# Query projection of 16-head cross-attention in three fp16 passes instead of one fp32 product

## The chip, the cores and the metric

The kernel runs on one core of a Trainium2 chip. One launch computes a whole twelve-stage model. The metric is the device time of the launch in microseconds (us). TensorE (PE) does the matrix products, VectorE (DVE) and ScalarE (ACT) the elementwise work, GpSimd (POOL) side work, and SyncE (SP) issues the transfers.

## The reference, cut to what matters

Three of the twelve stages (L0, L2 and L3 xattn) are the same cross-attention with different weights. Two batches of 128 tokens attend to 2048 context rows each. There are 16 query heads and 8 key heads, of 128 values each.

```
xn = layernorm(x)                                  # [2, 128, 256]
q = xn @ Wq;  k = ctx @ Wk;  v = ctx @ Wv          # k and v repeated for two heads each
scores = einsum('bhtd,bhsd->bhts', q, k) / sqrt(128)
attn = softmax(where(mask, scores, -inf))
x = x + einsum('bhts,bhsd->bhtd', attn, v) ... @ Wo
```

Between them stand nine other stages (state-space layers, other attentions, feed-forward layers). The last one, L3 ffn, has eight experts whose weights are quantised in advance, during the L2 and L3 xattn stages.

## The kernel before, in words

`xattn_layer` (lines 291 to 840) builds one cross-attention stage. It never forms k: the query of a head is multiplied by Wk's transpose (`qk_project`, L449), and the scores are that product against the transposed context, which stays in SBUF as an fp16 high part and an fp16 low part. A product with both parts takes three passes: high by high, high by low, low by high (`PARTS`, line 36).

The 16 heads go in four bodies (i = 0 to 3) of four heads. A head has two units, one per batch, so a body has eight units u = 0 to 7. Two heads share one key head and form a group (i, j), j = 0 or 1. In unit (i, u) PE does, in this order:

- `mix_high` (L475): high part of the probabilities by the low part of the values, 16 products of 128x128;
- `tail_out` (L523) of an earlier head, in odd units;
- `q_project` (L442) for group (i+1, 0) in u = 2 and (i+1, 1) in u = 6, of bodies 0 to 2: four fp32 products of 128x256, two trace records each;
- `scores` (L462) of unit u + 3: 12 products of 128x512 fp16;
- `tail_values` (L518) in even units, which waits for `oT` from DVE (L757);
- `mix_both` (L484): 16 products of 128x256 fp16;
- `qk_project` (L449) of the group, in u = 2 and 6.

The projections of (0, 0) and (0, 1) stand ahead of the bodies (lines 563 to 571), and after them PE has `scores` of units 0, 1 and 2 and nothing else before `mix_high` of unit 0.

DVE adds the mask, takes maxima (L742), inverts the sums (L752) and makes the low part of the probabilities (L766). ACT does the exponentials (L597), the high part (L612) and the copies of the projections out of PSUM (L587, L591).

The probabilities must be turned before they are mixed. That is done by transposing DMAs on SP's queue: `turn_high` (L379) and `turn_low` (L386) for each unit. SP executes its program in order, and in the same program it issues the weight loads: `load_q(i, j)` (L367, columns 0 to 639, Wq and Wk of a group) and `load_v` (L371). Each has a wait ahead of it, so whatever stands behind a wait of SP stands still until that wait ends. `turn_high` of unit u waits for `mix_both` of unit u - 2, since two buffers are used in turn; for u = 0 and 1 of body 0 it waits only for ACT's probabilities. Before, the loads stood so:

```
if u == 0 and not final:
    sp.wait_ge(s.qk_psum, 2 * i + 1)
    load_q(i + 1, 0)
if u == 4 and not final:
    sp.wait_ge(s.qk_psum, 2 * i + 2)
    load_q(i + 1, 1)
```

`qk_psum` counts finished `qk_project`s: group (i, j) makes it 2i + j + 1.

GpSimd in the L0 stage sets constants and makes the low part of the values (L702). In L2 and L3 it runs `experts_pool` (L3193): for each body one expert, whose first half is L3204 and L3207 (after DVE's L3153, in unit 0) and whose second half is L3211 to L3226 (after DVE's L3161, in unit 3).

Of the kernel before, what the change touches and what calls it, by code (L numbers as in the profile page):

```python
# [22 lines left out]
P = 128  # L23
# [46 lines left out]
def begin(nc, stack, dram):  # L70
    k = Shared()
    k.nc, k.dram = nc, dram

    def sb(name, shape, dt=F32):
        return stack.enter_context(nc.sbuf_tensor(name, shape, dt))

    k.x = sb("x", [P, B, D])
    k.xn = sb("xn", [P, B, D])
    k.xnT = sb("xnT", [P, DC, T])
    k.ident = sb("ident", [P, P])  # L80
    k.identb = sb("identb", [P, P], BF16)
    k.identh = sb("identh", [P, P], F16)
    k.ones = sb("ones", [P, P])
    k.zeros = sb("zeros", [P, 2 * D])
    k.zero = sb("zero", [P, 1])
    k.causal = sb("causal", [P, P])
    k.upper = sb("upper", [P, P])
    k.hm = sb("hm", [P, 16])
    k.wsum = sb("wsum", [P, 2])
    k.bits = sb("bits", [P, 2], I32)  # L90
    k.stats = sb("stats", [P, B, 6])
    k.mv = sb("mv", [P, B, 2])
    k.std = sb("std", [P, 2, B])
    k.rstd = sb("rstd", [P, 2, B])

    k.ctx = sb("ctx", [P, 2, B * KT, CD], F16)
    k.ctxT = sb("ctxT", [P, 2, B, CTX], F16)
    k.arena = [sb(f"arena{i}", [P, ARENA]) for i in range(2)]
    k.ps = stack.enter_context(nc.psum_tensor("ps", [P, 8, 512], F32))

    k.psh = k.ps[:].rearrange("p a n -> p (a n)").bitcast(F16).rearrange("p (a n) -> p a n", a=8)
    k.psi = k.ps[:].rearrange("p a n -> p (a n)").bitcast(I32).rearrange("p (a n) -> p a n", a=8)
    k.g = semaphores(nc, stack, "g", "x_loaded first_w0 first_w1 mask_loaded keys_loaded0 keys_loaded1 values_loaded0 values_loaded1 "
                               "keys_high0 keys_high1 keys_low0 keys_low1 values_high0 values_high1 values_low const_id const_zero const_ones const_copied "
                               "var_ready std_ready xn_ready xnT_psum xnT_ready dve_chain act_chain pool_chain "
                               "w_loaded0 w_loaded1 out_stored ln_chain "
                               "raw_loaded w_exp w_scaled w_bits w_added w_coded w_turned codes_loaded scale_rows")
    free = [i for i in range(256) if nc.free_contains(i)]
    k.turns = [range(max(free) + 1 - SEMS[0], max(free) + 1),
               range(max(free) + 1 - SEMS[0] - SEMS[1], max(free) + 1 - SEMS[0])]  # L110
    k.dve_n = k.act_n = k.pool_n = 0
    k.w_count = [0, 0]

    k.ln = k.xt = 0
    return k
# [175 lines left out]
def xattn_layer(k, name, slot, loaded, stage_loads):  # L291
# [8 lines left out]
    with ExitStack() as stack:  # L300
        def sb(nm, shape, dt=F32):
            return stack.enter_context(nc.sbuf_tensor(f"{name}_{nm}", shape, dt))
        s = semaphores(nc, stack, name, "wq0 wq1 wv0 wv1 out_done qT_psum qT_ready qk_psum qk_high qk_ready s_ready "
                 "s_read0 s_read1 p_ready r_raw r_ready p_high p_low t_hi0 t_hi1 t_lo0 t_lo1 mixed "
                 "oT_ready oh_psum oh_ready mask_ready last_psum last_hi last_lo0 last_lo1 oT_low", k.turns[slot])
        w = k.arena[slot][:, 0:2 * GW].rearrange("p (a n) -> p a n", a=2)
        bias = sb("bias", [P, B, CTX], BF16)
        anyone = sb("anyone", [P, B])
# [5 lines left out]
        pp = k.arena[slot][:, 2 * GW + 2 * CTX:2 * GW + 4 * CTX].bitcast(F16).rearrange("p (s a n) -> p s a n", s=2, a=2)  # L314
        pt = k.arena[slot][:, 2 * GW:2 * GW + 2 * CTX].bitcast(F16)\
            .rearrange("p (s a t q) -> p s a t q", s=2, t=KT, a=2)
        qT = sb("qT", [P, 2, T])
        qk = sb("qk", [P, 2, 2, 2, T], F16)
        mx = sb("mx", [P, 2, 2])
# [6 lines left out]
            weigh = Weigh(sb("round", [P, WE]), sb("exp", [P, FE // 2, WE // BLK]), sb("inv", [P, FE // 2, WE // BLK]))  # L326
        oT = sb("oT", [P, T])
        oh = sb("oh", [P, T])
        wq = [w[:, i, 0:2 * DC * HD].rearrange("p (h c d) -> p h c d", h=2, c=DC) for i in range(2)]
        wkT = [w[:, i, 512:640] for i in range(2)]  # L330
        wv = [w[:, i, 640:768] for i in range(2)]
        wo = [w[:, i, 768:768 + 2 * D].rearrange("p (h d) -> p h d", h=2) for i in range(2)]
# [30 lines left out]
        with nc.Block() as block:  # L363
            @block.sync
            def _(sp):
# [30 lines left out]
                def body(i, first, final):  # L396
                    for u in range(UNITS):
                        early = first and u < 2
                        if u == 0 and not final:
                            sp.wait_ge(s.qk_psum, 2 * i + 1)  # L400
                            load_q(i + 1, 0)
                        if u == 4 and not final:
                            sp.wait_ge(s.qk_psum, 2 * i + 2)
                            load_q(i + 1, 1)
                        if u == 3 and not first:
                            sp.wait_ge(s.out_done, BODY * i)
                            load_v(i, 1)
# [13 lines left out]
            def _(pe):  # L421
# [3 lines left out]
                keep_busy(k, 1, 3 if opening else 4, still)  # L425
                xT_tensor(k, pe, k.xn, 0, n)
                keep_busy(k, 1, 5, still)
                pe.wait_ge(g.xnT_ready, k.xt + 1)

                def q_project(i, j, first):  # L430

                    if first and opening:
                        pe.wait_ge((g.first_w0, g.first_w1)[j], 16)
                    elif first:
                        wait_weights(k, pe, slot, loaded)
                    else:
                        pe.wait_ge(wq_sem[j], 16 * i)
                    if not (first and j == 0):
                        pe.wait_ge(s.qk_ready, 2 * i + j)
                    for h in range(2):  # L440
                        for c in range(DC):
                            last = nc.tensor.matmul(PREP[:, h * T:(h + 1) * T], wq[j][:, h, c, :], k.xnT[:, c, :],  # L442
                                                    start=(c == 0), stop=(c == DC - 1))
                    last.then_inc(s.qT_psum, 1)

                def qk_project(i, j):
# [132 lines left out]
            @block.scalar  # L579
            def _(act):  # L580
                ln_scalar(k, act, n)
                xT_scalar(k, act, k.xnT, 0)
                nc.scalar.activation(unused[:], k.zero[:], ACT.Exp, bias=k.zero[:])

                def q_copy(i, j):
# [107 lines left out]

            @block.gpsimd
            def _(pool):
                if opening:
                    constants_pool(k, pool)
                    for b, done in enumerate((g.values_high0, g.values_high1)):
                        pool.wait_ge(done, 1)
                        for half in range(2):  # L700
                            at = slice(half * CTX // 2, (half + 1) * CTX // 2)
                            nc.gpsimd.tensor_tensor(rows_of(1, b)[:, at], raw_context(k, b)[1][:, at], rows_of(0, b)[:, at],  # L702
                                                    ALU.subtract).then_inc(g.values_low, 1)
                if experts is not None:
                    experts_pool(k, pool, weigh, experts)

            @block.vector
            def _(dve):
                if opening:
                    dve.wait_ge(g.x_loaded, 16)  # L710
                ln_vector(k, dve, k.x, k.xn, LN_EPS, n)
                if opening:
                    dve.wait_ge(g.mask_loaded, 16)
                else:
# [2475 lines left out]
    k.dve_n = chain.n  # L3190

def experts_pool(k, pool, w, first):  # L3193

    nc, g = k.nc, k.g
    chain = Chain(pool, g.pool_chain, k.pool_n)
    blocks = WE // PIECES // BLK

    for e in range(first, first + FE // 2):
# [6 lines left out]
        for j in range(PIECES):  # L3206
            nc.gpsimd.tensor_tensor(in_blocks(y[j]), in_blocks(y[j]), each_block(inv[j]), ALU.mult)\  # L3207
                .then_inc(g.w_scaled, 1)
        pool.wait_ge(g.w_bits, e + 1)
        for j in range(PIECES):  # L3210
            nc.gpsimd.tensor_scalar(y[j], y[j], E4M3_TOP, -E4M3_TOP, ALU.min, ALU.max)  # L3211
# [13 lines left out]
        for j in own:  # L3225
            nc.gpsimd.tensor_tensor(in_blocks(coded[j]), in_blocks(y[j]), each_block(ex[j]), ALU.mult)\  # L3226
                .then_inc(g.w_coded, 1)
    k.pool_n = chain.n

def turn_experts(k, sp, own):
# [523 lines left out]
```

## Time and profile before

| what | value |
|---|---|
| three timed runs | 1295.93, 1300.39, 1302.8 us, median 1300.39 |
| profiled execution, own time | 1297.31 us |
| its span in the trace | 1295.6 us |
| PE matmul busy | 1146.9 us, 89% of the span |
| DVE busy | 992.0 us, 77% |
| ACT busy | 860.9 us, 66% |
| POOL busy | 317.5 us, 25% |
| mean granted TensorE clock | 0.959 of full speed |

The span is 1.7 us shorter than the execution's own time, and that execution is 3.1 us below the median. The three cross-attention stages lie at about 3 to 240 us, 597 to 835 us and 970 to 1200 us.
### The profile page before, as it was taken

To read this page: it belongs to the slowest core of one execution; us is meant where nothing else is said; L and a number is where in the kernel's file an instruction comes from. 1 tells how busy PE (TensorE), PEld (TensorE's weight loads), DVE (VectorE), ACT (ScalarE), POOL (GpSimd) and SP (SyncE) were. 2 spreads that over 40 slices of the span, in tenths; PEclk is the share of its full clock that TensorE was granted. 3 is DMA by queue.
4 is the path that set the end of the run, shared out by engine and by line. 5 is a ranking of instruction groups with operands and counts; after the bars stand their busy time and mean duration, and the time that the engine had idled before them with its cause. 6 is when DMAs were issued, how large, how long until landed. Compare 5 with 4: busy or idle time off the path is not lost. (4 is left out here: it accounts for less than half of the span.)

```text
span 1295.6 us, 23108 instructions
## 1 busy us (share of the span) xinstructions
PE 1146.9 (89%) x8738; PEld 761.3 (59%) x8742; DVE 992.0 (77%) x1858; ACT 860.9 (66%) x1303; POOL 317.5 (25%) x353
## 2 busy tenths in 40 slices
PE   7999999848776887899899999887998999999987
PEld 3677676635322444486566666645874666666644
DVE  6788878297768883493899989776987998998654
ACT  5777778484454887422877777565976777777563
POOL 3000000100362000000172654502650456275200
PEclk8899999959986999899899999999998999999999
DMA  7999999201374000901899999514745999999600
GB/s 280 172 186 189 188 171 187 84 1 74 82 146 82 2 3 2 245 25 59 162 200 182 206 182 169 130 43 160 205 115 129 180 181 183 178 163 169 123 1 9
DMA packets 450833, 170.00 MB, mean 131 GB/s; under 512 B 437160, under 2 KB 437544, under 8 KB 449064
## 3 DMA queue, kind: packets, MB, share of 16 engines
q1 hardware_dynamic: 450736, 168.72, 62.3%
q8 instruction: 60, 0.98, 0.3%
q14 instruction: 37, 0.30, 0.1%
HBM read 58.84 MB, written 0.26 MB: 46 GB/s over the span
## 5 line engine op out<-in xcount | busy, mean ns | idle before, releaser
L462 PE MATMUL ps<-ctxT,L_xattn_qk 128*128 128x512 f16 x1152 | 270.3, 385 | 0.8 <-DVE L_xattn_mx L742 0.5
L766 DVE SCALAR_TENSOR_TENSOR arena<-L_xattn_sm,L_xattn_rr,arena 128x1024 f16<-128x1024 f32 x192 | 260.9, 1399 | 9.4 <-ACT arena L612 9.4
L597 ACT ACTIVATE L_xattn_sm<-L_xattn_sm,L_xattn_mx 128x2048 f32<-128x2048 f32 x96 | 192.3, 2003 | 75.6 <-DVE L_xattn_mx L742 73.9
L612 ACT ACTIVATE arena<-L_xattn_sm,L_xattn_rr 128x1024 f16<-128x1024 f32 x192 | 210.0, 1140 | 5.2
L462 PEld LDWEIGHTS ps<-ctxT,L_xattn_qk 128*128 128x128 f16 x1152 | 112.5, 99 | 130.1 <-issue 9.9
L484 PE MATMUL ps<-arena,ctx 128*128 128x256 f16 x1488 | 177.7, 273 | 0.0
L484 PEld LDWEIGHTS ps<-arena,ctx 128*128 128x128 f16 x1488 | 145.4, 98 | 31.9
L742 DVE CUSTOM_DVE_ANT_0 L_xattn_sm<-ps,L_xattn_bias 128x1024 f32<-128x1024 f32 x96 | 117.0, 1219 | 55.7 <-issue 55.5
L742 DVE CUSTOM_DVE_ANT_0 L_xattn_sm<-ps,L_xattn_bias,L_xattn_mx 128x1024 f32<-128x1024 f32 x96 | 123.2, 1284 | 2.4 <-DVE L_xattn_mx L742 2.1
L475 PE MATMUL ps<-arena,ctx 128*128 128x128 f16 x1488 | 100.8, 222 | 9.6 <-DMA arena<-arena 9.5
L475 PEld LDWEIGHTS ps<-arena,ctx 128*128 128x128 f16 x1488 | 92.3, 99 | 25.1 <-DMA arena<-arena 13.4
L2794 DVE TENSOR_REDUCE L_xattn_mx<-ps 128x1 f32<-128x512 f32 x128 | 81.0, 684 | 19.6 <-PE ps L2350 18.2
L180 PE MATMUL ps<-ctxT,identh 128*128 128x512 f16 x312 | 80.8, 394 | 8.6 <-PEq L363 2.5
L602 ACT ACTIVATE L_xattn_rr<-L_xattn_raw,L_xattn_anyone 128x1 f32<-128x1 f32 x96 | 28.2, 294 | 74.7 <-DVE L_xattn_raw L752 73.7
L2624 ACT ACTIVATE L_xattn_p<-ps,zero 128x512 f32<-128x512 f32 x84 | 53.1, 685 | 9.7 <-PE ps L2379 9.3
L180 PEld LDWEIGHTS ps<-ctxT,identh 128*128 128x128 f16 x312 | 29.6, 100 | 46.3 <-issue 22.5
L3211 POOL TENSOR_SCALAR arena<-arena 128x384 f32<-128x384 f32 x32 | 26.5, 827 | 119.9 <-DVE L_xattn_round L3161 118.4
L147 ACT ACT_TABLE_LOAD x10 | 12.8, 1283 | 63.7 <-PEq L892 20.3
L1940 PE MATMUL ps<-L_ffn_hTp,L_ffn_parts 128*128 128x256 f16 x408 | 51.1, 277 | 2.1 <-DVE L_ffn_parts L2041 2.1
L899 POOL MEMSET L_attn_xcp<- 128x524 f32 x1 | 0.5, 537 | 210.9 <-POOLq L363 210.9
L3212 POOL TENSOR_SCALAR L_xattn_round<-L_xattn_round 128x384 f32<-128x384 f32 x32 | 49.5, 1548 | 2.0
L3204 POOL TENSOR_TENSOR L_xattn_inv<-bits,L_xattn_exp 128x48 int32<-128x48 int32 x8 | 2.1, 266 | 190.5 <-DVE L_xattn_exp L3153 190.5
(585 smaller groups left out, 2082.7 us busy)
## 6 DMA issues: line engine op xcount, KB each, us to landing
L_ffn_ring<-in_L_ffn_experts SPq DMA_DIRECT2D x34, 384.0 KB, 3.6
arena<-in_L_xattn_w SPq DMA_DIRECT2D x36, 320.0 KB, 3.7
arena<-in_L_ffn_experts SPq DMA_DIRECT2D x8, 768.0 KB, 7.7
arena<-in_L_xattn_w SPq DMA_DIRECT2D x6, 640.0 KB, 6.5
arena<-arena SPq DMA_TRANSPOSE x193, 4.5
arena<-in_L_ffn_codes SPq DMA_DIRECT2D x1, 3072.0 KB, 11.2
arena<-in_L_attn_w SPq DMA_DIRECT2D x1, 2163.0 KB, 19.3
arena<-in_L_attn_w SPq DMA_DIRECT2D x2, 1026.0 KB, 5.1
```

The costliest lines, as they stand in the source:

```text
L180: k.nc.tensor.matmul(k.ps[:, bank, :], k.identh[:], k.ctxT[:, 0, 0, 0:512] if data is None else data, start=True, stop=True)
L462: last = nc.tensor.matmul(ps[:, at, :], qk[:, h // 2, qp, h % 2, b * P:(b + 1) * P], k.ctxT[:, cp, b, at * 512:(at + 1) * 512], start=(a = ...
L475: nc.tensor.matmul(O[h][:, b, 0, :], k.ctx[:, 1, b * KT + kt, :], pt[:, b, 0, kt, :], start=(kt == 0), stop=False, skip_group_check=True)
L484: last = nc.tensor.matmul(O[h][:, b, :, :], k.ctx[:, 0, b * KT + kt, :], pt[:, b, :, kt, :], start=False, stop=(kt == KT - 1), skip_group_ ...
L597: nc.scalar.activation(sm[:, u % 2, :], sm[:, u % 2, :], ACT.Exp, bias=mx[:, u % 2, 1:2], scale=-1.0, accum_out=rs[:, u % 2:u % 2 + 1]).th ...
L612: nc.scalar.mul(pp[:, u % 2, 0, at], sm[:, u % 2, at], rr[:, u % 2:u % 2 + 1]).then_inc(s.p_high, 1)
L742: nc.vector.tensor_tensor_reduce(sm[:, u % 2, half * 1024:(half + 1) * 1024], ps[:, 2 * half:2 * half + 2, :].rearrange("p a n -> p (a n)" ...
L766: nc.vector.scalar_tensor_tensor(pp[:, u % 2, 1, at], sm[:, u % 2, at], rr[:, u % 2:u % 2 + 1], pp[:, u % 2, 0, at], ALU.mult, ALU.subtrac ...
L1940: last = nc.tensor.matmul(gu(e)[:, half * T:(half + 1) * T], w13(e, wp)[:, c, half * MI:(half + 1) * MI], hTp[:, hp, c, :], start=(c == 0 ...
L2624: nc.scalar.activation(pt[step % 3][:, j, :, :].rearrange("p i q -> p (i q)"), ps[:, ST_BANK[piece % 3], :], ACT.Exp, bias=k.zero[:], scal ...
L2794: nc.vector.tensor_reduce(mx[:, G % 2, 2 * pair + which, at:at + 1], ps[:, bank, :], AX_X, ALU.max)\
L3212: last = nc.gpsimd.tensor_scalar(r[j], r[j], E4M3_LOW, ROUND, ALU.max, ALU.mult)
```

## The change: what it does, and the diff

- The normalised, transposed input is split into an fp16 high part (ACT, in place of the fp32 copy) and an fp16 low part (a new DVE subtraction out of PSUM) before the first projection.
- The query weights of each group are split into high and low fp16 parts in a new tile `wqh`, by a copy and a subtraction of 128x512 on GpSimd, eight groups per stage (`split_queries`).
- `q_project` does three fp16 passes (12 products of 128x256) and waits for GpSimd's `wq_low` and not for the load.
- `load_q` is issued earlier: (i+1, 1) in u = 0 and (i+2, 0) in u = 4, and (1, 0) and (1, 1) both in u = 0 of body 0. The waits ahead of them are those on `qk_psum` of the group that used the buffer before.
- In L2 and L3 the splits of later groups stand inside `experts_pool`: (e+1, 1) behind the scaling, (e+2, 0) at an expert's end (e counted within the stage).

```diff
@@ SyncE
+                        if u == 0 and first:
+                            sp.wait_ge(s.qk_psum, 1)
+                            load_q(1, 0)
                         if u == 0 and not final:
-                            sp.wait_ge(s.qk_psum, 2 * i + 1)
-                            load_q(i + 1, 0)
-                        if u == 4 and not final:
                             sp.wait_ge(s.qk_psum, 2 * i + 2)
                             load_q(i + 1, 1)
+                        if u == 4 and i + 2 <= LASTI:
+                            sp.wait_ge(s.qk_psum, 2 * i + 3)
+                            load_q(i + 2, 0)
@@ TensorE
-                pe.wait_ge(g.xnT_ready, k.xt + 1)
+                pe.wait_ge(g.xn_low, {"L0_xattn": 1, "L2_xattn": 2, "L3_xattn": 3}[name])
                 def q_project(i, j, first):
...
+                    pe.wait_ge(s.wq_low, 2 * i + j + 1)
...
                         for c in range(DC):
-                            last = nc.tensor.matmul(PREP[:, h * T:(h + 1) * T], wq[j][:, h, c, :], k.xnT[:, c, :],
-                                                    start=(c == 0), stop=(c == DC - 1))
+                            for a, (wpart, xp) in enumerate(PARTS):
+                                last = nc.tensor.matmul(PREP[:, h * T:(h + 1) * T], wq[j][:, wpart, h, c, :],
+                                                        xh[:, xp, c, :], start=(c == 0 and a == 0),
+                                                        stop=(c == DC - 1 and a == len(PARTS) - 1))
@@ ScalarE
-                xT_scalar(k, act, k.xnT, 0)
+                act.wait_ge(g.xnT_psum, k.xt + 1)
+                nc.scalar.copy(xh[:, 0, :, :].rearrange("p c t -> p (c t)"), ps[:, 0, :]).then_inc(g.xnT_ready, 1)
@@ GpSimd
+                def split_queries(chain, i, j):
+                    if i == 0 and opening:
+                        pool.wait_ge((g.first_w0, g.first_w1)[j], 16)
+                    elif i == 0:
+                        wait_weights(k, pool, slot, loaded)
+                    else:
+                        pool.wait_ge(wq_sem[j], 16 * i)
+                        pool.wait_ge(s.qT_psum, 2 * i + j - 1)
+                    chain(nc.gpsimd.tensor_copy(wqh[:, j, 0, :], w[:, j, 0:2 * DC * HD]))
+                    nc.gpsimd.tensor_tensor(wqh[:, j, 1, :], w[:, j, 0:2 * DC * HD], wqh[:, j, 0, :], ALU.subtract)\
+                        .then_inc(s.wq_low, 1)
                 if opening:
                     constants_pool(k, pool)
+                chain = Chain(pool, g.pool_chain, k.pool_n)
+                split_queries(chain, 0, 0)
+                if opening:
                     for b, done in enumerate((g.values_high0, g.values_high1)):
+                        if b:
+                            split_queries(chain, 0, 1)
                         pool.wait_ge(done, 1)
...
+                    for i in range(1, LASTI + 1):
+                        for j in range(2):
+                            split_queries(chain, i, j)
+                else:
+                    split_queries(chain, 0, 1)
+                    split_queries(chain, 1, 0)
+                    experts_pool(k, pool, chain, weigh, experts, split_queries)
@@ VectorE
                 ln_vector(k, dve, k.x, k.xn, LN_EPS, n)
+                dve.wait_ge(g.xnT_ready, k.xt + 1)
+                nc.vector.tensor_tensor(xh[:, 1, :, :].rearrange("p c t -> p (c t)"), ps[:, 0, :],
+                                        xh[:, 0, :, :].rearrange("p c t -> p (c t)"), ALU.subtract).then_inc(g.xn_low, 1)
@@ experts_pool, for e in range(first, first + FE // 2)
                 .then_inc(g.w_scaled, 1)
+        if e % 4 < LASTI:
+            split_queries(chain, e % 4 + 1, 1)
         pool.wait_ge(g.w_bits, e + 1)
...
                 .then_inc(g.w_coded, 1)
+        if e % 4 + 1 < LASTI:
+            split_queries(chain, e % 4 + 2, 0)
```

## Rows read from the trace of the kernel before

**Rows 1.** Windows in L0 and L2: PE, PEld, DVE, ACT, POOL busy; clock, DMA share, GB/s.

```profile
45.00:208.00 163.00, 163.00 (x1234) 114.62 (x1233) 133.14 (x244) 126.60 (x163) 0.00 (x0) 1.00 1.00 183
630.00:793.00 163.00, 160.59 (x1204) 111.27 (x1202) 147.12 (x245) 122.60 (x157) 83.95 (x75) 1.00 0.98 186
```

**Rows 2.** PE's timeline (start, length in us), L0 stage, units 1 to 4 of body 0.

```profile
46.12 1.91 PE L484 MATMUL ps<-arena,ctx 128*128 128x256 f16 x16
47.87 1.06 PE L475 MATMUL ps<-arena,ctx 128*128 128x128 f16 x16
48.76 1.95 PE L442 MATMUL ps<-xnT,arena 128*128 128x256 f32 x8
50.54 2.75 PE L462 MATMUL ps<-ctxT,L_xattn_qk 128*128 128x512 f16 x12
...
55.31 1.02 PE L449 MATMUL ps<-L_xattn_qT,arena 128*128 128x512 f32 x2
...
62.32 0.89 PE L475 MATMUL ps<-arena,ctx 128*128 128x128 f16 x13
```

**Rows 3.** Timeline of the opening of L2: SP's first turn, and PE.

```profile
617.07 1.68 SPq L379 DMA_TRANSPOSE arena<-arena  x1
...
617.56 1.13 PE L449 MATMUL ps<-L_xattn_qT,arena 128*128 128x512 f32 x2 [1.31 <-ACT L_xattn_qT L587]
621.63 1.89 PE L475 MATMUL ps<-arena,ctx 128*128 128x128 f16 x16 [2.94 <-DMA arena<-arena]
```

**Rows 4.** The same timeline in the opening of L0.

```profile
29.92 2.04 SPq L379 DMA_TRANSPOSE arena<-arena  x1
...
30.42 1.12 PE L449 MATMUL ps<-L_xattn_qT,arena 128*128 128x512 f32 x2 [0.23 <-ACT L_xattn_qT L587]
```

**Rows 5.** Window behind that wait in L2; columns as in Rows 1.

```profile
621.60:627.60 6.00, 5.97 (x27) 3.27 (x28) 4.18 (x7) 5.42 (x6) 0.00 (x0) 0.51 1.05 182
```

**Rows 6.** SP: query loads; landing of all 93 high turns; one turn behind a load.

```profile
L367 SPq DMA_DIRECT2D arena<-in_L_xattn_w x18: 328/928/1290, 17.3 to 1121.6; - x18
...
DMA to landing us min/median/max: 4.3/4.6/6.5
...
L379 SPq DMA_TRANSPOSE arena<-arena x1: 3146/3146/3146, 134.4 to 134.4; - x1
...
DMA to landing us min/median/max: 6.4/6.4/6.4
```

**Rows 7.** Timeline of L2's and L0's starts; DVE's L727 by line (ns min/median/max).

```profile
600.08 0.59 ACT L196 COPY xnT<-ps 128x512 f32<-128x512 f32 x1 [1.72 <-PE ps L190]
...
602.88 0.59 ACT L587 COPY L_xattn_qT<-ps 128x512 f32<-128x512 f32 x1 [0.61 <-PE ps L442]
...
14.61 0.58 ACT L587 COPY L_xattn_qT<-ps 128x512 f32<-128x512 f32 x1
...
L727 DVE SCALAR_TENSOR_TENSOR L_xattn_qk<-ps,L_xattn_qk x24: 675/682/692, 18.0 to 1159.9; 128x512 f16<-128x512 f32 x24
```

**Rows 8.** Timeline of L2, body 0, unit 2 and the unit behind it.

```profile
634.15 4.19 POOL L3207 TENSOR_TENSOR arena<-arena,L_xattn_inv 128x384 f32<-128x384 f32 x4
...
636.34 3.09 DVE L766 SCALAR_TENSOR_TENSOR arena<-L_xattn_sm,L_xattn_rr,arena 128x1024 f16<-128x1024 f32 x2
...
639.42 0.40 DVE L757 SCALAR_TENSOR_TENSOR L_xattn_oT<-ps,L_xattn_oT 128x256 f32<-128x256 f32 x1
...
639.98 0.41 PEld L518 LDWEIGHTS ps<-L_xattn_oT,arena 128*128 128x128 f32 x2
...
642.36 2.48 DVE L766 SCALAR_TENSOR_TENSOR arena<-L_xattn_sm,L_xattn_rr,arena 128x1024 f16<-128x1024 f32 x2
```

**Rows 9.** GpSimd: groups by line nearest in shape to a split; L0's opening (timeline).

```profile
L2291 POOL TENSOR_TENSOR L_xattn_p<-L_xattn_p 128x512 f16<-128x512 f32 x16 | 18.9, 1184 | 0.0
L2290 POOL COPY L_xattn_p<-L_xattn_p 128x512 f16<-128x512 f16 x16 | 10.0, 626 | 32.7 <-ACT L_xattn_p L2554 32.5
...
19.89 9.31 POOL L702 TENSOR_TENSOR ctx<-arena,ctx 128x1024 f16<-128x1024 f32 x4 [15.62 <-ACT ctx L675]
```

More of the change, by code:

```diff
@@ L104, in begin @@
                                "keys_high0 keys_high1 keys_low0 keys_low1 values_high0 values_high1 values_low const_id const_zero const_ones const_copied "
-                               "var_ready std_ready xn_ready xnT_psum xnT_ready dve_chain act_chain pool_chain "
+                               "var_ready std_ready xn_ready xnT_psum xnT_ready xn_low dve_chain act_chain pool_chain "
                                "w_loaded0 w_loaded1 out_stored ln_chain "
@@ L304, in xattn_layer @@
                  "s_read0 s_read1 p_ready r_raw r_ready p_high p_low t_hi0 t_hi1 t_lo0 t_lo1 mixed "
-                 "oT_ready oh_psum oh_ready mask_ready last_psum last_hi last_lo0 last_lo1 oT_low", k.turns[slot])
+                 "oT_ready oh_psum oh_ready mask_ready last_psum last_hi last_lo0 last_lo1 oT_low wq_low", k.turns[slot])
         w = k.arena[slot][:, 0:2 * GW].rearrange("p (a n) -> p a n", a=2)
@@ L316, in xattn_layer @@
             .rearrange("p (s a t q) -> p s a t q", s=2, t=KT, a=2)
+        xh = flat(k.xnT[:]).bitcast(F16).rearrange("p (a c t) -> p a c t", a=2, c=DC)
+        wqh = sb("wqh", [P, 2, 2, 2 * DC * HD], F16)
         qT = sb("qT", [P, 2, T])
@@ L328, in xattn_layer @@
         oh = sb("oh", [P, T])
-        wq = [w[:, i, 0:2 * DC * HD].rearrange("p (h c d) -> p h c d", h=2, c=DC) for i in range(2)]
+        wq = [wqh[:, i, :, :].rearrange("p a (h c d) -> p a h c d", h=2, c=DC) for i in range(2)]
         wkT = [w[:, i, 512:640] for i in range(2)]
@@ L427, in _ @@
                 keep_busy(k, 1, 5, still)
-                pe.wait_ge(g.xnT_ready, k.xt + 1)
+                pe.wait_ge(g.xn_low, {"L0_xattn": 1, "L2_xattn": 2, "L3_xattn": 3}[name])
                 def q_project(i, j, first):
[L432 to L437, printed above, removed]
+                    pe.wait_ge(s.wq_low, 2 * i + j + 1)
                     if not (first and j == 0):
@@ L703, in _ @@
                                                     ALU.subtract).then_inc(g.values_low, 1)
-                if experts is not None:
-                    experts_pool(k, pool, weigh, experts)
+                    for i in range(1, LASTI + 1):
[5 more added lines that the diff above has]
+                    experts_pool(k, pool, chain, weigh, experts, split_queries)
+                k.pool_n = chain.n
             @block.vector
@@ L3190, in expert_end, with experts_pool @@
     k.dve_n = chain.n
-def experts_pool(k, pool, w, first):
+def experts_pool(k, pool, chain, w, first, split_queries):
     nc, g = k.nc, k.g
-    chain = Chain(pool, g.pool_chain, k.pool_n)
     blocks = WE // PIECES // BLK
@@ L3227, in experts_pool @@
                 .then_inc(g.w_coded, 1)
-    k.pool_n = chain.n
+        if e % 4 + 1 < LASTI:
+            split_queries(chain, e % 4 + 2, 0)
 def turn_experts(k, sp, own):
```

## The prediction
> **What bounds the kernel now.** I read the windows first. In the middle of the L0 cross-attention PE is busy 163.00 of 163.00 us at full clock, DVE 133; in L2 PE has 160.59 of 163 and DVE 147 [rows 1]. So inside these three stages PE is the bound, with about 1.5% of idle time in L2 and L3, and whatever PE issues there costs its own spacing. The DMA engines' share is 1.00 there too, so transfers have little room. The second view is PE's timeline [rows 2], where one block starts as the last ends. The third is the opening of a stage [rows 3, 4]. There PE runs dry: after L449 it has nothing until the first turned probabilities land, and L475 waits 2.94 us for that DMA. The first L475 follows SP's first turn by 4.56 us (617.07 to 621.63), so in an opening SP's issue time sets PE's restart.
>
> **The projections in the bodies (gain).** From L442's start to L462's start are 50.54 - 48.76 = 1.78 us for the fp32 form. The nearest fp16 row of the same width is L484: 16 products from 46.12 to 47.87, 109 ns each [rows 2]. Twelve of these are 1.31 us. A projection saves 0.47 us. There are two per body in bodies 0 to 2 of three stages, 18 in all, each between busy PE blocks: 18 x 0.47 = 8.5 us. Bounds: nothing, if what follows waits anyway, and 24 x 0.47 = 11.3 if the six opening projections counted too.
>
> **The six opening projections.** Group (0, 1) saves nothing: L449 behind it waits for ACT's copy [rows 3]. In L0 this projection has a new wait, on a split that stands behind two of the four L702, so from about 19.89 + 9.31 / 2 = 24.5 us on. By L2290 and L2291 a split is 0.63 + 1.18 = 1.8 us [rows 9], ready at 26.4. The projection and three units' scores must be done when L449's input comes at 30.42 [rows 4], and 26.4 + 1.31 + 12 x 0.216 (the spacing of 2.75 us of L462) = 30.3 just fits: 0, with 0.5 as the upper bound. Group (0, 0) gets DVE's subtraction in its way: ACT ends at 600.67, DVE adds about 0.68 by L727 with the same output shape and PSUM source, PE takes 1.31 and 0.2 of latency, so ACT's copy starts near 602.9 to 603.1, against 602.88 [rows 7]. I take +0.2 in L2 and in L3. In L0 that copy starts only at 14.61, behind ACT's key copy, so split and subtraction are covered there; were the keys earlier, 2 us would show. The splits of L2 and L3 for (0, 0) run while DVE normalises; their weights are loaded a stage ahead. Sum: +0.4.
>
> **SP's new wait in the opening (loss).** Body 0, unit 0 now has a wait for qk_psum >= 2 and load (1, 1) ahead of turn_high(0, 0). Two is reached when the L449 of group (0, 1) ends: 617.56 + 1.13 = 618.69 in L2, 30.42 + 1.12 = 31.54 in L0 [rows 3, 4]. A load takes SP 0.33 us on an idle queue, 0.93 by the median [rows 6]. The turn then goes out near 619.1 in place of 617.07, and 32.0 in place of 29.92: 2.0 us later. I take the same for L3, whose lines are L2's. The 320 KB of the load are in flight with it: the turn at 134.36 right behind a load took 6.4 us to land, the median turn 4.6 [rows 6]; I add 0.3, bounded by 0 and 1.8. Behind the waiting instruction stand all turns of the stage, and PE waits for the first. Its idle time of 2.94 becomes 5.2 us. Cost 3 x 2.3 = +6.9 us, and nothing of that is won back, since PE is the bound afterwards. Bounds 3 and 12, which includes the clock: behind the wait PE works 6 us at 0.51 of full speed, the lower level (1.2 GHz) [rows 5]. If full clock comes back at the same moment as before, half of the delay falls on slow time and the cost is 3.5; if it comes back one such stretch's half later (3 us at half speed), each opening costs 1.5 more.
>
> **SP's waits in the bodies (loss).** In unit 4 of bodies 0 and 1, and unit 0 of bodies 1 and 2, SP waits for the L449 of two units before, which stands directly behind the L484 that the next turn waits for anyway. Before, that load was issued in SP's free time. Now: L449 ends 55.31 + 1.02 = 56.33, the load is 0.93, so the turn goes at 57.3; with 4.6 to landing 61.9, with 6.4 it is 63.7. PE wants it at 62.32 [rows 2, 6]. So a usual landing has 0.4 us of slack and a slow one is 1.4 late. With a load right ahead of each I take 0.2 us on the mean, 12 times: +2.4, bounded by 0 and 12 x 1.0 = 12. The load in unit 4 of body 2 disappears, worth nothing: its turn has slack.
>
> **GpSimd beside DVE.** A split costs 1.8 us [rows 9], 24 are 43 us on an engine with 25% of its time used; no wait for wq_low is late in a body, since the loads are two to four units earlier than the use. What it slows is DVE: L766 takes 3.09 us beside GpSimd's L3207 and 2.48 without [rows 8]. In L2, unit 2 of body 0, L757 ends at 639.82 and PE's L518 starts at 639.98 [rows 8]. That 0.16 us of slack means that of the 0.47 saved 0.3 is waited there; and the new split (1, 1) directly behind L3207 lengthens the same L766 by up to 0.3 more. I take 0.6 for that unit and 0.1 for body 2's, in two stages: +1.4, bounded by 0 and 4. The Trainium skill's GPSIMD Engine Reference, section Key points, states that GpSimd shares its SBUF interfaces with VectorE and that a DVE instruction with two SBUF inputs contends; by that rule the LN and score passes (L742, one input in PSUM) would be untouched. The trace agrees as far as L766 goes. In L0 DVE has 30 us of idle time in 163 [rows 1], so there it costs nothing.
>
> **The sum.** -8.5 + 0.4 + 6.9 + 2.4 + 1.4 = +2.6 us. Against the profiled execution's own 1297.3 us that is 1299.9; that execution is 3.1 below the median of the runs, so on the median 1300.4 the forecast is **1303.0 us**. A measurement of this kernel tells a change from none at about 0.5%, 6.5 us; by that the forecast is no change.
>
> **The rivals.**
> *Late turns (slower).* The place is SP's program order at the twelve waits in the bodies. Its price is the landing of a turn with 320 KB ahead of it. It decides from the point where issue to landing exceeds 62.32 - 57.3 = 5.0 us. For it: DMA share 1.00 [rows 1], 6.4 us behind a load, maximum 6.5 [rows 6]. Against it: median 4.6. At 6.0 us each is 1.0 late, 12 us instead of 2.4: 1303.0 + 9.6 = 1312.6. Chance 0.23.
> *The opening is nearly free (faster).* The first landing is not what holds PE: the later turn falls where the clock is low anyway, the slack of 0.4 us holds at the twelve places, and DVE is not slowed. Then -8.5 + 0.4 + 1.5 = -6.6, 1293.8 us. For it: 6 us at 0.51 clock [rows 5]. Against it: 2.94 us of idle time put down to exactly that DMA, and nothing else for PE to do. Chance 0.08.
> *The fp16 form is not 109 ns a product.* Each product needs its own weight load, twelve in place of eight records; if the spacing were L442's own 0.22 us, a projection would take 2.7 us and 18 would cost 16 us, 1328. L484 has the same shape and one load per product at 109 ns, so I give it 0.02. The Trainium skill's page TensorE: Matmul & The Clock Gate, section Back-to-back issue gap, puts an isolated product of 256 columns at 256 / 2.4 + 2.5 = 109 ns, which is the trace's number.
> *The forecast,* openings 2.3 us each and small waits at the turns: 0.67.
>
> **How the numbers follow.** The forecast case spans 1297 to 1309 by its bounds taken together (openings 3.5 to 10, turns 0 to 5), and most of it lies within 6.5 us of 1300.4; about a twentieth of all lies above and belongs to slower. Faster by over 0.5% is 0.07, slower 0.25, no change 0.68. The range of 8 in 10 goes from 1294 to the middle of the late-turn case, 1312.
>
> **What would show it.** Right: L442's successor takes 12 records at 109 ns, 1.3 us from start to the next L462; the first L475 of each stage waits about 5 us on the DMA in place of 3, its turn issued 0.3 to 0.5 us after L449's end with the load between; in the bodies the turns of units 4 and 0 go out about 1.7 us after L449's start. Wrong: first turns at the old distance behind ACT's L612; L475 waiting over 1 us on a DMA at many of the twelve places (late turns); PE's wait for wq_low visible; or L518's waits for L757 grown past 1.5 us each.

## The result, and the profile after

The changed kernel takes 1310.46 us (median of 5 runs, 1307.10 to 1312.76); the kernel before, on the same chip, 1299.33. The ratio is 1.0080 with a 95% interval of 1.0055 to 1.0105: slower by about 10 us, where the forecast said 2.6 slower and called it no change (less than 0.5%). The profiled execution has a span of 1308.7 us against 1295.6, at a mean granted clock of 0.954 against 0.959. So the traces differ by 13.1 us, 3 more than the timed runs. Of the 13.1, the three cross-attention stages hold 9.2 (710.4 us before, 719.6 after) and the nine stages that the change doesn't touch 3.9; the experiments show what a granted clock does to such stages.

The page of the changed kernel: the engines' busy time, and L477, which is L475 of before (columns: busy us, mean ns | idle us ahead of it, releaser). Line numbers move with each edit: here L443, L451, L464 and L520 are L442, L449, L462 and L518 of before, and `oT`, on which L520 waits, comes from L787 in place of L757.

```profile
PE 1141.4 (87%) x8834; PEld 756.1 (58%) x8838; DVE 1000.4 (76%) x1861; ACT 860.7 (66%) x1303; POOL 375.3 (29%) x401
L477 PE MATMUL ps<-arena,ctx 128*128 128x128 f16 x1488 | 100.8, 222 | 23.6 <-DMA arena<-arena 23.6
```

The same group before, from that kernel's page:

```profile
L475 PE MATMUL ps<-arena,ctx 128*128 128x128 f16 x1488 | 100.8, 222 | 9.6 <-DMA arena<-arena 9.5
```

PE does 5.5 us less work and waits 14 us more for turned probabilities. Where it does so stands in PE's list of waits (us in total, times, longest), after:

```profile
PE ps L477 <- DMA arena<-arena: 23.6, 10, 6.0
...
PE ps L190 <- DVE xn L139: 8.6, 5, 2.2
```

Three of the ten are the openings, 6.04, 5.99 and 5.37 us; before they were 3.06, 2.94 and 2.97. The others add to 6.2. The second line is the normalisation, 4.1 us before.

**The projection.** Timeline of the changed kernel, L0, unit 2 of body 0; it answers to [rows 2].

```profile
49.47 1.47 PE L443 MATMUL ps<-xnT,L_xattn_wqh 128*128 128x256 f16 x12
50.78 1.46 PE L464 MATMUL ps<-ctxT,L_xattn_qk 128*128 128x512 f16 x6
```

50.78 - 49.47 = 1.31 us, twelve products at 109 ns. It was 1.78.

**The opening.** Timeline of L2's opening, SP's queue first, as in [rows 3]:

```profile
619.82 0.33 SPq L369 DMA_DIRECT2D arena<-in_L_xattn_w  x1
620.19 3.18 SPq L381 DMA_TRANSPOSE arena<-arena  x1
...
618.66 1.13 PE L451 MATMUL ps<-L_xattn_qT,arena 128*128 128x512 f32 x2 [1.68 <-ACT L_xattn_qT L590]
625.77 1.03 PE L477 MATMUL ps<-arena,ctx 128*128 128x128 f16 x8 [5.99 <-DMA arena<-arena]
```

The load goes out just after L451's end at 619.79, the turn 0.37 us behind it, so 1.53 us after L451's start. Before, the turn stood 0.49 us ahead of that start (617.07 against 617.56): 2.0 us later, as predicted. But from issue to PE's restart it now takes 5.58 us in place of 4.56. SP's own issue is longer, 3.18 us against 1.68, and the load's 320 KB are in flight with the turn. Which of the two makes the turn late is not shown, and neither has a fixed price: in L0 the landing is 1.0 us later as well, in L3 0.4, and in e3 below L2's first turn, behind the same load and issued in 3.22 us, lands only 0.2 later than before.

**The start of a stage.** L2, timeline of GpSimd, DVE and PE; it answers to [rows 7].

```profile
596.92 1.16 POOL L709 TENSOR_TENSOR L_xattn_wqh<-arena,L_xattn_wqh 128x512 f16<-128x512 f32 x1
...
597.32 0.78 DVE L135 TENSOR_SCALAR rstd<-mv 128x2 f32<-128x2 f32 x1
...
598.67 1.67 DVE L139 TENSOR_SCALAR xn<-x,mv,rstd 128x256 f32<-128x256 f32 x2
598.72 1.15 POOL L709 TENSOR_TENSOR L_xattn_wqh<-arena,L_xattn_wqh 128x512 f16<-128x512 f32 x1
...
600.40 0.66 PE L190 MATMUL ps<-ident,xn 128*128 128x128 f32 x4 [2.18 <-DVE xn L139]
...
601.71 0.69 DVE L740 TENSOR_TENSOR xnT<-ps,xnT 128x512 f16<-128x512 f32 x1 [1.37 <-ACT xnT L585]
```

The kernel before had for the same two operations:

```profile
597.86 0.17 DVE L135 TENSOR_SCALAR rstd<-mv 128x2 f32<-128x2 f32 x1
...
598.59 0.74 DVE L139 TENSOR_SCALAR xn<-x,mv,rstd 128x256 f32<-128x256 f32 x2
```

L135 works on two numbers a partition and takes 0.78 us: it starts inside GpSimd's subtraction L709 and ends at 598.10, with it (596.92 + 1.16 = 598.08). L139 gets 0.93 us longer, beside the second L709. L3 has the same two lengths in its trace. The forecast had put these splits at nothing.

**Turns in the bodies.** All 93 high turns of the changed kernel, from issue to landing; before, in [rows 6], 4.3/4.6/6.5.

```profile
DMA to landing us min/median/max: 4.2/4.6/7.5
```

The median stands still and the tail grows. At the twelve places of the prediction five waits are left, 4.0 us in all (the longest 1.77, L2, unit 4 of body 1). The other two of the ten, 1.52 and 0.68, stand at turns of L2 and L0 that the prediction didn't name; the first is behind the experts' load.

### The profile page after: what moved, and what is told of

Its sections match the earlier page's. It is cut to its first block and busy times, and to the rows that moved or that the text cites. A ratio compares the mean times of both kernels' runs of the same rounds, so it can differ in the third digit from the quotient of the medians.

```text
span 1308.7 us, 23363 instructions
## 1 busy us (share of the span) xinstructions
PE 1141.4 (87%) x8834; PEld 756.1 (58%) x8838; DVE 1000.4 (76%) x1861; ACT 860.7 (66%) x1303; POOL 375.3 (29%) x401
## 5 line engine op out<-in xcount | busy, mean ns | idle before, releaser
L464 PE MATMUL ps<-ctxT,L_xattn_qk 128*128 128x512 f16 x1152 | 269.2, 384 | 0.8 <-DVE L_xattn_mx L772 0.5
L464 PEld LDWEIGHTS ps<-ctxT,L_xattn_qk 128*128 128x128 f16 x1152 | 112.0, 99 | 127.0 <-issue 8.5
L477 PE MATMUL ps<-arena,ctx 128*128 128x128 f16 x1488 | 100.8, 222 | 23.6 <-DMA arena<-arena 23.6
L477 PEld LDWEIGHTS ps<-arena,ctx 128*128 128x128 f16 x1488 | 92.0, 99 | 40.0 <-DMA arena<-arena 28.2
L708 POOL CAST L_xattn_wqh<-arena 128x512 f16<-128x512 f32 x24 | 24.6, 1024 | 172.8 <-DMA arena<-in_L_xattn_w 116.2
L525 PE MATMUL ps<-arena,L_xattn_oh 128*128 128x256 f32 x180 | 48.7, 393 | 0.0
## 6 DMA issues: line engine op xcount, KB each, us to landing
arena<-in_L_ffn_codes SPq DMA_DIRECT2D x1, 3072.0 KB, 11.5
```

The source lines that it names most:

```text
L464: last = nc.tensor.matmul(ps[:, at, :], qk[:, h // 2, qp, h % 2, b * P:(b + 1) * P], k.ctxT[:, cp, b, at * 512:(at + 1) * 512], start=(a = ...
L477: nc.tensor.matmul(O[h][:, b, 0, :], k.ctx[:, 1, b * KT + kt, :], pt[:, b, 0, kt, :], start=(kt == 0), stop=False, skip_group_check=True)
```

## The experiments

Three parts were in question: SP's order of loads and turns (theory S), GpSimd's splits beside DVE's normalisation (G), and what the fp16 passes are worth in full bodies (P against D, DVE's chain). The ratios are to the kernel before, timed beside each kernel: medians 1299.57 us for e1 to e4, 1298.60 for e5 to e8, 1300.50 for e9 to e11.

**e1_open.** Load (1, 1) of body 0 one unit later.

```diff
-                        if u == 0 and not final:
+                        if u == (1 if first else 0) and not final:
```

> The changed kernel, with only the load of group (1, 1) moved in body 0 from ahead of unit 0's turns to behind them. Theory S (SP's order holds PE): the first mix of each stage waits 3 us again in place of 5.4 to 6.0, and the time falls by 7 to 9 us, to 1302 or so. Theory G (GpSimd's splits cost the time, in the normalisation and beside DVE): the time stays within 3 us of 1310.

**e2_later_loads.** All the earlier loads but (1, 0) one unit later, so that none stands ahead of a turn that its own wait holds up; (1, 0) stays in unit 0 of body 0, where its wait is long over.

```diff
-                        if u == 0 and not final:
+                        if u == 1 and not final:
...
-                        if u == 4 and i + 2 <= LASTI:
+                        if u == 5 and i + 2 <= LASTI:
```

> The changed kernel with all of these loads one unit later: (i+1, 1) in unit 1 and (i+2, 0) in unit 5, behind the turns of units 0 and 4. Theory S: the openings give 7 to 9 us as in the run before, the twelve places in the bodies 3 to 4 more, together 10 to 13, so 1298 to 1300, and no turn of units 0 and 4 is late. Theory G: within 3 us of 1310. If the landing behind a load is what matters and not the wait, the late turns move to units 1 and 5 and only the 7 to 9 us of the openings come back.

**e3_split_after_ln.** The changed kernel, with GpSimd's first split behind the normalisation in L2 and L3.

```diff
                 chain = Chain(pool, g.pool_chain, k.pool_n)
+                if not opening:
+                    pool.wait_ge(g.xn_ready, n + 1)
                 split_queries(chain, 0, 0)
```

> The changed kernel with one wait more: in L2 and L3 GpSimd starts its splits only when DVE has normalised. Theory G: DVE's L135 and L139 take 0.17 and 0.74 us again in place of 0.78 and 1.67, PE's first transpose is 1.5 us earlier in two stages, and the split is still ready before the first projection; 3 us less, up to 5 with the clock of L3's first projection, so 1306 to 1307. Theory S alone: no change beyond 1 us.

**e4_both.** e2 and e3 together.

> Later loads and splits behind the normalisation together. Both theories in sum: 13 to 16 us less than 1310, so 1294 to 1297, which is below the kernel before (1299.3) by 3 to 5 us, the projections' gain of 8.5 less what remains: the new subtraction, GpSimd beside DVE, slower turns. If GpSimd beside DVE in the bodies costs more than 3 us it ends at or above the kernel before.

Measured: e1 1305.14 us (ratio to before 1.0045, 1.0027 to 1.0064), e2 1305.33 (1.0031, 1.0013 to 1.0049), e3 1306.36 (1.0054, 1.0036 to 1.0073), e4 1300.66 (0.9998, 0.9982 to 1.0015). Against the expectations, e3 came out as theory G said; e1 and e2 gave some 5 us where S promised 7 to 9 and 10 to 13, and e4 ended 4 to 7 us above what the two were to give together. In e1 the first waits of the three stages are 3.20, 2.93 and 2.98 us, as before. The medians of e1 and e2 don't tell the twelve places apart from nothing, though in e2's trace no wait is left at them. Where part of the gain went can be read from PE's waits: from the changed kernel to e2 those for turns fall from 23.6 to 13.2 us, but those for DVE's `oT` rise from 7.0 to 9.2 and those of L451 for ACT from 8.5 to 10.3. Late turns seem to have covered waits that PE would have had anyway. In e3's trace the normalisation is as short as it was:

```profile
601.15 0.17 DVE L135 TENSOR_SCALAR rstd<-mv 128x2 f32<-128x2 f32 x1
...
601.88 0.73 DVE L139 TENSOR_SCALAR xn<-x,mv,rstd 128x256 f32<-128x256 f32 x2
```

So both causes are real. S is worth 5 us (the changed kernel to e2) or 5.7 (e3 to e4), G 4.1 (to e3) or 4.7 (e2 to e4); S is clear by the intervals in both steps. For G they overlap from the change to e3 and just touch from e2 to e4; its case rests on both steps together and on the traces, where the hold of 1.55 us ahead of L190 in L2 is there with the early splits and gone without them. Together they undo the whole net loss: the interval of e4 holds 1. What follows is also a new question. If the losses are gone and 18 projections save 0.47 us each, why is e4 not 8 us faster than before?

**e5_before_new_loads.** The kernel before with the change's places of the loads alone: fp32 projections, no splits.

```diff
+                        if u == 0 and first:
+                            sp.wait_ge(s.qk_psum, 1)
+                            load_q(1, 0)
                         if u == 0 and not final:
-                            sp.wait_ge(s.qk_psum, 2 * i + 1)
-                            load_q(i + 1, 0)
-                        if u == 4 and not final:
                             sp.wait_ge(s.qk_psum, 2 * i + 2)
                             load_q(i + 1, 1)
+                        if u == 4 and i + 2 <= LASTI:
+                            sp.wait_ge(s.qk_psum, 2 * i + 3)
+                            load_q(i + 2, 0)
```

> The kernel before with the change's load schedule alone; projections stay fp32, GpSimd has no splits. Theory S: it alone makes the kernel before slower, by what its undoing won (6.4 us, 0.5%) or a little more, 1305 to 1308, with 5 to 6 us of waiting at the first mix of each stage. If the loads hurt only together with the splits (GpSimd waits for them): no change, 1299 to 1301.

1310.24 us, ratio 1.0079 (1.0051 to 1.0108), 2 us above what theory S gave: the order on SP's queue by itself costs as much as the whole change. Its trace has first waits of 5.35, 5.52 and 5.79 us, in PE's list of waits:

```profile
PE ps L478 <- DMA arena<-arena: 18.1, 7, 5.8
```

**e10_before_late_loads.** e5 with those loads one unit later (u = 1 and u = 5), as in e2.

> The kernel before (projections of one fp32 pass, no splits) with the change's earlier loads, each issued one turn later: (i+1,1) at u = 1 and (i+2,0) at u = 5. Against e5_before_new_loads, which has the change's places and stood at +0.79%, it takes away SP's waits ahead of the first turns. Theory S (SP's order is the loss, 2.5 to 3 us an opening): first mix waits back at 3.0 to 3.7, 6 to 10 us less than e5, ratio 0.999 to 1.002. Against e11 it then prices the whole fp16 part (passes, splits, subtraction): by the prediction's step (a) e11 is 4 to 8 us faster than this kernel; if splits, DVE's subtraction and the ends of the bodies eat the gain, they are equal. Rival (the loads as such hold up the turns, wherever they are issued): ratio stays at 1.005 or more.

1301.16 us, ratio 1.0004 (0.9983 to 1.0026), first waits 3.04, 2.94 and 2.98. Loading three units earlier than before costs nothing that the runs can tell; loading ahead of a turn, behind a wait, costs 9 us (e5 against e10). The rival (the loads hold up the turns wherever they are) falls.

**e6_one_pass.** e4 with one of the three passes; the products with the low parts of weights and input are left out.

```diff
-                            for a, (wpart, xp) in enumerate(PARTS):
+                            for a, (wpart, xp) in enumerate(PARTS[:1]):
```

> The version with later loads and splits behind the normalisation, with one pass of the projection (high by high) in place of three; it leaves out the two products with the low parts. 8 products of 0.109 us less in 18 projections are 15.7 us. Theory P (PE is the bound in all three stages): 14 to 16 us less, about 1286. Theory D (in L2 and L3 DVE's chain to L757 takes over, PE then waits at tail_values): in L0 6 x 0.87 = 5.2 us, in L2 and L3 half of 10.5 or less, so 6 to 10 us, 1291 to 1295, and tail_values waits grow from 4 us a stage to 7 or 8.

1286.56 us, ratio 0.9898 (0.9869 to 0.9928). Eight products fewer are 0.87 us a projection; 24 are 21 us, and 13 to 14 came (the difference of the ratios or of the medians). In L0, bodies 1 and 2 fell from 51.59 us each in e4 to 50.32 and 49.84; the same bodies of L3 only from 53.58 to 52.86 and 52.78. The result lies between theory P's 15.7 and theory D's 6 to 10, nearer to P, and 1.9 us of it are waits for turns (12.7 in e4, 10.8 here). PE's waits for `oT` grew from 9.5 us in e4 to 12.2. PE bounds all stages, L2 and L3 not fully: in these bodies of L3 0.38 of 0.87 us a projection came.

**e7_no_body_splits.** e4 without the 18 splits of the bodies; groups (1, 0) to (3, 1) are projected with the split weights of groups (0, 0) and (0, 1), PE waiting for the loads.

```diff
                 def split_queries(chain, i, j):
+                    if i:
+                        return
```

> The same version without the 18 splits of the bodies; it leaves them out, so that later groups are projected with the split weights of groups (0, 0) and (0, 1). Theory G2 (GpSimd beside DVE in the bodies costs the missing gain): 3 to 5 us less than 1300.7, the gain showing in L2 and L3 bodies. Theory D (it is DVE's own chain, whatever GpSimd does): within 1.5 us of 1300.7.

1299.68 us, ratio 0.9997 (0.9973 to 1.0021), against e4's 1300.66: the 18 splits beside DVE in the bodies can't be told from nothing.

**e11_both_tuned.** e4 with load (1, 1) of body 0 in unit 2 and the loads of experts 2 and 3 in unit 2, away from the query load.

```diff
-                        if u == 1 and not final:
+                        if u == (2 if first else 1) and not final:
...
-                        if experts == 0 and u == 5 and i < 2:
+                        if experts == 0 and u == 2 and i < 2:
```

> e4_both with two more moves on SP's queue: in the first body of each stage the load (1,1) is issued at u = 2 (L0's second turn waited 1.37 us behind it in e4_both), and the loads of experts 2 and 3 in L2 at u = 2 in place of u = 5 (a turn of L2 waited 1.58 us behind load_q and load_experts). Theory S: both waits go, 1.4 us in L0 and 1.5 in L2 (not more than 0.3 left each), so 2 to 3 us under e4_both, median 1297 to 1300 here, ratio 0.996 to 0.999. Rival (DVE's chain ends the bodies, so that a turn's wait is taken back by the waits of tail_values for DVE): the waits go but tail_values' grow from 4.0 us, and the time stays at e4_both's, ratio 0.999 to 1.001. Rival (turns of the experts' loads moved only): another turn of L2 waits 1.5 us behind them, and L2's bodies are as long as in e4_both.

1298.45 us, ratio 0.9979 (0.9959 to 0.9999), 2.2 us below e4 and 2.7 below e10; the intervals overlap in both cases, so neither step is certain. The waits did go: the second turn of L0 and the turn of L2 that was 1.58 us late behind the experts' load are on time, and a wait of 0.44 in L2 is new.

e10 and e11 have the same order of loads but for these moves, so they price the fp16 part where PE is at full clock. Windows over bodies 1 and 2 of L0, then of L3 (busy us of PE, PEld, DVE, ACT, POOL; clock, DMA share, GB/s), e10:

```profile
88.60:193.70 105.10, 105.10 (x795) 73.81 (x794) 85.22 (x157) 81.04 (x105) 0.00 (x0) 1.00 0.99 181
...
1052.44:1160.25 107.81, 106.30 (x794) 73.70 (x792) 97.63 (x163) 80.89 (x105) 55.06 (x51) 1.00 0.97 178
```

and e11:

```profile
88.30:191.50 103.20, 103.20 (x810) 72.73 (x809) 85.19 (x157) 80.83 (x105) 6.86 (x6) 1.00 1.02 187
...
1053.00:1160.12 107.12, 104.77 (x811) 72.45 (x809) 97.08 (x163) 80.92 (x105) 67.85 (x59) 1.00 0.99 179
```

Four projections lie in each window. In L0 they bring 1.90 us, 0.47 each, the prediction's figure. In L3 they bring 0.69, 0.17 each. PE's waits in L3's window, e10 and then e11:

```profile
PE ps L521 <- DVE L_xattn_oT L760: 1.5, 4, 0.5
```

```profile
PE ps L520 <- DVE L_xattn_oT L789: 2.0, 4, 0.5
PE ps L451 <- ACT L_xattn_qT L590: 0.4, 2, 0.2
```

0.9 us of the 1.9 is given back, 0.5 waiting for the same DVE result and 0.4 for ACT's copy; for the last 0.3 the trace shows no single wait. In e7 the two lines read 2.0 and 0.4 as well, so it is not the splits that make DVE late; DVE is busy 97 us of 107 without them. GpSimd's other work is not ruled out. L0, in whose window PE waits for nothing, has no experts; L3 has them, with 55 us of GpSimd in e10's window and 12.4 us more of DVE. Part of these is L769 (L766 of before), the low part of the probabilities, in e10's window of L0 and then of L3:

```profile
L769 DVE SCALAR_TENSOR_TENSOR arena<-L_xattn_sm,L_xattn_rr,arena 128x1024 f16<-128x1024 f32 x33 | 40.9, 1280 | 0.0
...
L769 DVE SCALAR_TENSOR_TENSOR arena<-L_xattn_sm,L_xattn_rr,arena 128x1024 f16<-128x1024 f32 x33 | 48.6, 1513 | 0.0
```

That is 7.7 us, and DVE's own instructions for the experts are 5.8 more. That the experts' work is what puts DVE's chain into PE's way is therefore likely; no run here leaves it out.

**e8_l0_only.** The change in L0 alone, with loads at u = 2 (body 0), 1 and 5; L2 and L3 as before.

> The change in L0 alone, with its loads behind the turns (unit 2 in body 0, then 1 and 5); L2 and L3 as in the kernel before. By the bodies of the traces L0 gives 6 x 0.47 = 2.8 us and nothing is lost in L2 and L3: 1296 to 1297, ratio 0.998. If L0's opening pays for the new pass it stays at 1299 to 1300.

1302.79 us, ratio 1.0025 (1.0007 to 1.0043), slower than either expectation. L0's bodies 1 and 2 are 51.59 us each against 52.53, yet the kernel is not faster. In its trace the three cross-attention stages take 709.7 us against 710.4 before, and the nine others 596.1 against 585.2. Its L3 stage, whose code is the old one, needed 27.03 us to the first mix in place of 24.87. The window of its first 6 us, e8 and then before:

```profile
973.50:979.50 6.00, 5.94 (x14) 2.73 (x15) 4.27 (x9) 2.85 (x4) 0.00 (x0) 0.50 0.81 295
```

```profile
969.80:975.80 6.00, 5.32 (x24) 3.24 (x25) 4.28 (x9) 3.74 (x5) 0.00 (x0) 1.00 0.82 290
```

The same code ran at the lower level there, 1.2 GHz, with 14 records of matmuls in the time of 24.

**e9_before_again.** The kernel before, once more, to see what belongs to the execution.

> The kernel before, unchanged, executed and timed as if it were another kernel. It asks what one profiled execution is worth. If the lengths of the stages that the change doesn't touch are a matter of the kernel, this profile shows them as the first one did (fine_xattn stage 189.5 us, L2_attn 50.6, half-clock total 107 us). If they are a matter of the execution, at least one of them is longer here (195 or more for fine_xattn, 52 to 55 for L2_attn, a total of 115 to 140), and the even result of e4_both is then made of a gain in the three changed stages against the first profile (L0 -2.4 us, L3 -0.5, L2 +0.5) and of stretches of lower clock elsewhere. The ratio should be 1.000 with an interval of about 0.002 to each side: that is what 5 rounds can tell from nothing.

1298.75 us, ratio 0.9992 (0.9973 to 1.0011). The profiled execution is 1.8 us shorter than the first, and the difference is not spread evenly. The first body of L0 is 52.06 us in it, 53.98 in the first: windows of 54 us from its start, first and second execution.

```profile
34.60:88.60 54.00, 54.00 (x391) 37.20 (x392) 42.39 (x78) 41.02 (x52) 0.00 (x0) 0.95 1.01 181
```

```profile
33.60:87.60 54.00, 53.30 (x411) 37.25 (x412) 45.10 (x81) 43.64 (x55) 0.00 (x0) 1.00 1.01 183
```

And a stage that the change doesn't touch, the one with the largest swing: before, first execution, and e4.

```profile
330.00:519.50 189.50, 143.27 (x1915) 69.40 (x1914) 138.99 (x289) 128.32 (x235) 38.47 (x57) 0.92 0.27 53
```

```profile
327.60:524.90 197.30, 152.72 (x1915) 71.47 (x1914) 138.59 (x289) 128.16 (x235) 38.32 (x57) 0.87 0.27 51
```

The same 1915 records of matmuls, DVE as busy as ever, and 7.8 us more at a clock of 0.87 in place of 0.92. In e9 this stage took 191.2. e4's profiled span of 1301.7 is longer than before's 1295.6 by 6.1, and this stage alone holds more than that. Of the signs that e9's expectation named for a matter of the execution, one came (L2_attn: 52.5 against 50.7). The stage above (fine_xattn) stayed below 195, and the time at half clock was 93 us in e9 against 107 in the first execution, less and not more.

What stays open: in the traces the three cross-attention stages take 705.3 us in e11 against 710.8 in e10, 5.5 less (the openings take back 0.6 of a larger gain), and the medians give 2.7; and e8 should not be slower than before. Stretches of lower clock can hide as much: the nine other stages take 595.1 us in e11 against 591.2 in e10. Over all traces these nine take 585 and 586 us in the two executions of the kernel before and 589 to 598 in those of the eleven other kernels. That speaks for the kernel rather than chance, but one execution each doesn't show it, and no run shows the cause.

## Why the prediction was right and wrong

The sign of its sum and the main mechanism were right, and 1310.46 lies in the range; the size was not, +2.6 against some +10 by the ratio. By its own mark of 0.5%, the forecast of no change, to which it gave 0.68, did not come: +0.80% is its "slower", at 0.25. That the time lies in the range is in part luck. The forecast case was to end at 1309; the range reaches 1312 only because it was drawn out to the middle of the late-turn case, which is not what happened.

- *Projections in the bodies (-8.5): right per instruction, too large as a sum.* The form costs 109 ns a product and 1.31 us. In L0 six projections bring 0.47 each. In L3's full-clock bodies they bring 0.17. The prediction held that PE bounds L2 and L3 because its idle time is 1.5%, and took off 1.4 us in the term for GpSimd. But four waits for DVE in two bodies, 1.5 us in all in e10, mean that PE meets DVE's chain twice a body, and part of what it saves ahead of such a wait is waited there. By these rates 6 x 0.47 + 12 x 0.17 = 4.9. The term is mis-sized by 3.6, or by 2.2 with the 1.4 of the GpSimd term, half of which was meant for this.
- *SP's new wait in the openings (+6.9): mechanism right, size short.* The issue came 2.0 us later, as worked out. The landing cost 1.0 in L0 and L2 and 0.4 in L3, where the prediction took 0.3 from the range of 0 to 1.8. The first waits grew by 2.98, 3.05 and 2.40: 8.4 us.
- *The opening projections (+0.4): wrong.* The step that failed is "The splits of L2 and L3 for (0, 0) run while DVE normalises", counted at nothing. L190 comes 1.56 us later after the stage's start (4.15 against 2.59 from DVE's L123). DVE's subtraction adds 0.5 ahead of the projection, which is 0.47 shorter: in e4 and e11, where the splits wait, L2's first mix comes 24.94 us after the stage's start against 24.85, so for the subtraction the +0.2 was enough. In the changed kernel stage start to first mix grew from 24.85 to 29.52 in L2 and from 24.87 to 30.07 in L3, of which the SP wait is 3.05 and 2.40. The 1.6 left in L2 is as long as L190's delay. The 2.8 left in L3 holds more than that, since the clock was lower there (0.86 against 0.96 to the first mix); e5, which has no splits, needed 29.84 us in L3. e3's median is 4 us below the change's. The prediction quoted half of a rule for it: DVE instructions with two SBUF inputs. L135 and L139 have one tensor input each and were held all the same. The Trainium skill's page SBUF — State Buffer, section Who interferes with whom, has the other half: a tensor_scalar can run in a mode that uses the pair of ports that DVE and GpSimd share, and then the one that comes second stands still until the other's instruction ends. The trace agrees for L135, which ends with L709; L139 was recorded as starting 0.05 us ahead of the L709 that it ends behind. In which mode the two ran, no run here shows. In L0 a sign of being wrong that the prediction named did come: L443 of group (0, 1) waits 0.64 us for GpSimd's split. Nothing came of it, as PE still waits 0.3 us for ACT ahead of L451.
- *The twelve turns (+2.4): about right.* Five waits, 4.0 us. Its rival, late turns at 1312.6, lies nearer to the measured time, but not for its reason: it wanted 1.0 at each of twelve places. The waits at other turns, 2.2 us against 0.6 before, are in no term.
- *GpSimd beside DVE in the bodies (+1.4): half right.* That part of the saving is waited at L518 is what e11 shows, though in L3 too and at four places in two bodies. The other half, that the splits lengthen DVE's work, doesn't show: without the 18 splits the time is the same (e7), and so are PE's waits for DVE in L3's bodies.
- *Nothing won back in the opening.* Mostly so, but the parts don't add. e5 has the openings' waits and only 0.2 us at the twelve places, and stands at +11.6 us on the median (+10.3 by the ratio), its three first waits being 7.7 us longer; taking them out of the changed kernel brought 5, part of which is the waits for DVE and ACT that the late turns had covered. The prediction had named the clock as what could move it, 1.5 us an opening, and traces of one kernel do differ by 2 us there.

A sum with the measured terms: -4.9 + 8.4 + 4 + 4.0 = +11.5, in which the 4 is e3's. The ratio says 10.4, the three stages in the traces 9.2.

## What to carry to other kernels

A load that is moved, with its wait, ahead of a transfer for which an engine stands idle can cost twice: here 2.0 us by the wait in front of it, and 0.4 to 1.0 by the later landing. Issue it one unit later, behind that transfer; here that was worth the whole loss of e5, and the load was still in time. Before work is given to an idle GpSimd, look at which short DVE instructions on the path run beside it, not only at long ones. And where PE already meets another engine's chain twice a body, if only for a few tenths, price a saving on PE in that stage by half or less (here 0.17 of 0.47 us, and in e6 0.38 of 0.87).

## What the runs showed of the hardware

- A DVE tensor_scalar of 128x2 took 0.78 us in place of 0.17 beside a GpSimd subtraction, and two of 128x256 took 1.67 in place of 0.74.
- The issue of a stage's first turn right behind a load of 320 KB takes SP 3.2 to 3.8 us in the changed kernel in place of 1.7 to 2.0, and it lands 1.0, 1.0 and 0.4 us later in the three stages.
- One kernel, executed twice, differs by 1.9 us in one body and by 1.8 in another stage, as the granted clock falls (0.95 against 1.00, 0.93 against 0.97). Across kernels an untouched stage swings by 7.8 us. A sum of a few us can't be read from one pair of spans. Windows that both stand at 1.00 are steadier: L0's bodies 1 and 2 are 52.53 us each in both executions of the kernel before and in e10.
